# Layer 0 of a two-layer image kernel: VectorE's closing sum and statistics of each strip's second output half are moved one step later in its own instruction order

## What is computed

```python
def _L0_conv_ref(x, w_hidden, b_hidden, w_dw, b_dw, w_proj, b_proj, ln_w, ln_b):
    hidden = jnp.einsum('bchw,oc->bohw', x, w_hidden) + b_hidden[None, :, None, None]
    hidden = depthwise_3x3(hidden, w_dw) + b_dw[None, :, None, None]
    q, k, v = jnp.split(hidden, 3, axis=1)                  # 128 channels each
    q_fft = jnp.fft.rfft2(_to_patches(q))                   # patches of 8 by 8
    k_fft = jnp.fft.rfft2(_to_patches(k))
    out = _from_patches(jnp.fft.irfft2(q_fft * k_fft, s=(8, 8)))
    out = layernorm_over_channels(out) * ln_w + ln_b
    return jnp.einsum('bchw,oc->bohw', v * out, w_proj) + b_proj[None, :, None, None]

x = x + _L0_conv_ref(_gn(x), ...)      # _gn: group norm, 32 groups of 2 channels
x = x + _L1_conv_ref(_gn(x), ...)      # layer 1 needs the group statistics of layer 0's output
```

## Time and profile before

| what | before |
|---|---|
| median of 3 runs | 9162.08 us |
| the profiled execution's own time | 9166.47 us |
| its span | 9164.7 us |
| layer 0's loop (about 216 to 6476 us of the span) | 6260 us, 128 strips |
| TensorE busy, whole span | 8542.7 us (93%) |
| VectorE busy | 7484.3 us (82%) |
| ScalarE busy | 6350.6 us (69%) |
| GpSimd busy | 4819.6 us (53%) |
| mean granted TensorE clock | 0.985 of full speed |

### The profile page before, as it was taken

How to read it: one execution, slowest core, us unless ns; L and a number is a source line. 1 busy time by engine, 2 the same in 40 slices (tenths; PEclk the granted TensorE clock), 3 DMA queues, 4 the chain that set the end, 5 groups by cost and what they waited for, 6 DMA issues and landing times. The chain is left out here.

```text
span 9164.7 us, 170682 instructions
## 1 busy us (share of the span) xinstructions
PE 8542.7 (93%) x57838; PEld 4864.3 (53%) x57838; DVE 7484.3 (82%) x9864; ACT 6350.6 (69%) x8676; POOL 4819.6 (53%) x2752
## 2 busy tenths in 40 slices
PE   0999999999999999999999999999887999999999
PEld 0666666666666666666666666666432333333333
DVE  4788788788888878878887777778767999999999
ACT  0777777677777767777776777777406888888888
POOL 1444434344344344444443444434207999999999
PEclk9999999999999999999999999999998999999999
DMA  6122222222222222222212122122394555555555
GB/s 141 47 61 65 50 61 63 54 61 50 65 61 50 65 54 58 65 50 61 65 46 53 43 50 51 45 48 51 85 234 96 120 119 118 119 118 121 119 120 117
DMA packets 618296, 715.70 MB, mean 78 GB/s; under 512 B 44382, under 2 KB 577348, under 8 KB 594352
## 3 DMA queue, kind: packets, MB, share of 16 engines
q1 hardware_dynamic: 618160, 713.88, 33.4%
HBM read 549.03 MB, written 164.70 MB: 78 GB/s over the span
## 5 line engine op out<-in xcount | busy, mean ns | idle before, releaser
L633 PE MATMUL banks<-w_hi,hi_lo 128*128 128x256 f16 x18432 | 2407.1, 277 | 87.0 <-DVE hi_lo L935 87.0
L633 PEld LDWEIGHTS banks<-w_hi,hi_lo 128*128 128x128 f16 x18432 | 1760.3, 100 | 926.2 <-issue 523.7
L591 POOL TENSOR_TENSOR u_im<-q_im,k_swap 128x512 f32<-128x512 f32 x512 | 652.0, 1273 | 1834.4 <-ACT q_im L829 1747.5
L1442 POOL TENSOR_TENSOR part_sum<-part_sum,prod 128x1024 f32<-128x1024 f32 x660 | 1561.3, 2366 | 53.1
L967 DVE SCALAR_TENSOR_TENSOR v_s<-banks,tap_w,v_s 128x512 f32<-128x512 f32 x2048 | 1534.7, 749 | 54.6 <-ACT v_s L818 0.3
L1471 PE MATMUL banks<-z,conv_w 128*128 128x512 f32 x3128 | 1575.7, 619 | 0.0
L803 ACT ACTIVATE qk<-banks,inv_wscale 128x512 f32<-128x512 f32 x1024 | 706.4, 690 | 1221.2 <-PE banks L633 1215.7
L594 POOL TENSOR_TENSOR u<-u,u_im 128x512 f32<-128x512 f32 x512 | 726.4, 1419 | 1069.6 <-DVE u L944 1069.6
L633 PE MATMUL banks<-w_lo_pair,hi_pair 128*128 128x256 f16 x6144 | 1017.7, 275 | 0.0
L600 POOL TENSOR_TENSOR u<-u,u_mean 128x512 f32<-128x512 f32 x512 | 533.0, 1041 | 797.5 <-DVE u_mean L975 797.5
L944 DVE TENSOR_TENSOR u<-q_re,banks 128x512 f32<-128x512 f32 x512 | 349.6, 683 | 636.0 <-ACT q_re L831 635.7
(11 more groups left out here) (252 smaller groups left out, 15735.4 us busy)
## 6 DMA issues: line engine op xcount, KB each, us to landing
xr<-in_x_dram SPq DMA_DIRECT2D x258, 640.0 KB, 9.2
xb<-y_scratch SPq DMA_DIRECT2D x268, 320.0 KB, 4.7
xa<-y_scratch SPq DMA_DIRECT2D x268, 256.0 KB, 5.3
x_res<-in_x_dram SPq DMA_DIRECT2D x258, 256.0 KB, 4.0
out_dram<-res SPq DMA_DIRECT2D x258, 256.0 KB, 3.3
y_scratch<-ys SPq DMA_DIRECT2D x256, 256.0 KB, 3.9
yc<-y_scratch SPq DMA_DIRECT2D x256, 256.0 KB, 5.5
xs<-in_x_dram SPq DMA_DIRECT2D x92, 512.0 KB, 7.2
```

The lines of the kernel that those rows point to most:

```text
L591: nc.gpsimd.tensor_tensor(u_im[:], q_im[:], k_swap[:], ALU.mult).then_inc(u_made, 1)
L633: r = pe.matmul(out, px, w, start=n == 0, stop=n == 13)
L1442: nc.gpsimd.tensor_tensor(part_sum[:], prod[0][:] if n == 0 else part_sum[:], prod[n + 1][:], ALU.add)\
```

## The change

`finish` is cut in two behind L991. Its last two instructions, L994 and L996, with their waits and the signal `pair_ready`, become a function `output`. In step 0 of a strip (first half of the output) `output` is called right behind `finish`, as before. In step 2 (second half) it is no longer called there: it is called at the end of the next step, step 3, behind the last six `taps`. `high_stacks`, `both_stacks`, `product`, `times_v`, `taps` and `means` of step 3 now stand ahead of it. The end of the loop calls both halves in the order of before.

```diff
@@ -990,6 +990,13 @@
                     v.tensor_tensor(t_n[:], b_y[:], rs[:], ALU.mult)
                     v.scalar_tensor_tensor(out, b_var[:].rearrange("p (c r) -> p r c", r=R), b_proj[:, 0:1],
                                            x_res[sb_][:, :, GCOL * m:GCOL * m + GCOL], ALU.add, ALU.add).then_inc(fin_read, 1)
+
+                def output(i, k):
+
+                    m = ((k - 4) % 4) // 2
+                    sb_ = ((k - 4) // 4) % 2
+                    done = i * 4 + (k - 2) // 2
+                    out = ys[sb_][:, :, GCOL * m:GCOL * m + GCOL]
                     v.wait_ge(fin_read, done)
                     v.tensor_tensor(out, out, t_n[:].rearrange("p (c r) -> p r c", r=R), ALU.add).then_inc(fin_step, 1)
                     v.wait_ge(fin_step, done)
@@ -1067,8 +1074,12 @@
                             taps(i, k, 2, 8)
                         if stats and k == 4:
                             x_chunk(i)
+                        if k % 4 == 3 and not (first and k < 5):
+                            output(i, k - 1)
                         if k % 2 == 0 and not (first and k < 4):
                             finish(i, k)
+                        if k % 4 == 0 and not (first and k < 4):
+                            output(i, k)
                         if k % 4 == 2:
                             high_stacks(s, b)
                         if k % 4 == 0:
@@ -1079,8 +1090,10 @@
                     times_v(NB, 0, True)
                     means(NB, 0)
                     finish(NB, 0)
+                    output(NB, 0)
                     times_v(NB, 1, True)
                     finish(NB, 2)
+                    output(NB, 2)
```

## The result

The changed kernel takes 8866.99 us (median of 4 runs, 8863.69 to 8872.17) against 9162.82 us: ratio 0.9673, interval 0.9661 to 0.9684. That is 296 us less.

What follows compares the result with a forecast made beforehand. TensorE was taken to bound layer 0's loop. VectorE's chain shortens by 4.44 - 2.50 + 0.87 - 1.00 = 1.81 us; over 126 strips, less 2.7 us, that saves 225.4 us: 8937 us, range 8895 to 8988.

Steps and rivals of the forecast that it cites:

- What bounds layer 0: Layer 0's loop goes at TensorE's pace except for waits at inverse and the stacks, 2.08 us a strip.
- What is taken out, 4.44 us: VectorE, step 2: without L994 and L996 ahead of the stacks, L918 comes 4.44 us earlier.
- the hold handed to L918, 2.50: VectorE, step 2: GpSimd's L581 now holds L918 as it held L994, costing 2.50 us.
- L922 freed, 0.87: VectorE's L922 would be through before GpSimd's L591 and no longer held, giving back 0.87 us.
- the second hold on a copy, 1.00: GpSimd's L591 falls into L924 and the VectorE copy behind it waits, costing 1.00 us.
- What TensorE gets of it as wait: Step 3's chain moves with L944: TensorE's waits shrink by 1.81 us a strip, leaving 0.27 us at inverse.
- The new place, SyncE's queue: Output behind step 3's taps and pair_ready about 15.7 us later, delaying queued loads and store: cost 0 for both.
- Image boundaries: In 3 strips TensorE waits 5.6 us for VectorE's L1029; 0.9 us each off the gain, 2.7 us.
- TensorE gains 1.81 us per strip; the most it could is 2.08: TensorE in layer 0's loop: gain of 1.81 us a strip, capped by its waits of 2.08 us.
- Rival 1: The second hold does not happen, g is 2.81 us, both TensorE waits vanish: 8903 us; chance 0.2.
- Rival 2: Holds pile up: L918 3.37, copy 1.27 us, 9078 us; or L994 loses to L591, 9019 us; chance 0.11.
- Rivals 3 and 4: TensorE waits the same for ScalarE, 9162 us, chance 0.03; or late input load, 9477 us at 40 us landing, chance 0.03.

Runs made afterwards that it cites:

- e9: Changed kernel with the L918 pair (edge rows) taken out of step 2 and put at the end of step 1: 8833 us, ratio 0.9635.
- e11: e9 with the next image's variance computed in step 0 ahead of finish, output and masks, three times a run: 8817 us, ratio 0.9623.
- e12: Changed kernel with the late add (end of step 3) working on one of 64 columns, output not the reference's: 8860 us, ratio 0.9671.
- e6: Changed kernel with the first half's add and statistics moved too, to the end of step 1 behind its taps: 8863 us, ratio 0.9675.
- e2: Kernel before with only the statistics (L996) and their signal moved to the end of step 3, the add L994 left in step 2: 9030 us, ratio 0.9852.
- e5: Changed kernel with three useless GpSimd products of 1.04 us each ahead of step 3's less_mean: 9174 us, ratio 1.0007.
- e10: Kernel before, output untouched, with only the L918 pair moved to the end of step 1: 8939 us, ratio 0.9753.
- e1: Kernel before with the second half's output put behind high_stacks, still in step 2: 9131 us, ratio 0.9957.

## Why the prediction was wrong, point by point

*What bounds layer 0*: right. With the two waits gone, e9 and e11 leave TensorE nearly no wait in the loop.

*What is taken out, 4.44 us; the hold handed to L918, 2.50; L922 freed, 0.87; the second hold on a copy, 1.00*: right in kind and close in size. Measured are 2.42 (3.81 less 1.39), 0.87 and 0.98 (1.67 less 0.69). Sum 1.91 us against 1.81, and the chain in the timeline is 1.92 shorter. That L581 keeps its turn hung on a narrow margin, and here the forecast had luck: L581 starts 0.09 us ahead of L918, where it started 0.10 us ahead of L994. In nearly all strips it is 0.09 or 0.10 us.

*What TensorE gets of it as wait*: right. 228.5 us of idle time went in the loop (222 over the span), 225 were forecast. The 0.27 us left at `inverse` in each strip, 34 us in all, is 33.8 us. *The new place, SyncE's queue*: cost 0, right within 15 us, as e12, e6 and e2 show. *Image boundaries*: 0.9 us each was taken off, 1.5 is lost in wait.

*Where it failed*: the step "TensorE gains 1.81 us per strip; the most it could is 2.08". It takes TensorE's busy time as fixed, so that no more than its waits could be gained, and from that came both the forecast and the low end of 8895. But the wait of 1.8 us cost more than itself: in 42 of the strips TensorE's clock fell to half for some 3.4 us behind it, 1.65 to 1.8 us of lost time each, and with the wait these went too, all but one. e5 shows the link from one side (the wait alone brings them back), e10 from the other (another edit that shortens the wait drops them). That term is 72 us, put at nothing: 222 us of idle and 72 of busy time are the 294 us by which the profiled span is shorter. The idle part was forecast within 3 us.

The sign stood in the rows of before and was not read: the row of the loop's busy times gives a granted clock of 0.99, one hundredth of 6260 us, 63 us, or with the rounding anything from 31 to 94. In the kernel after the same figure is 1.00. The list of what would make the forecast wrong looked at waits alone.

Rival 1 (both waits vanish, 8903) and the others asked only how much wait goes. Rival 2's second form (L591 wins against the moved add) did not happen: the add arrives first. Its first form (both holds longer) did not happen either: they are 2.42 and 0.98. Rivals 3 and 4 did not come up: ScalarE still waits for TensorE, and L790 in the loop for no load.

## What to carry to other kernels

Where TensorE bounds a stage and has short regular waits, look for products of one shape that take longer behind some of the waits, and at the granted clock of the stage in hundredths: here a wait of 1.8 us cost another 1.7 us where the clock fell, about twice its length, and removing part of it (from 1.8 to 1.4 us here) can already bring the whole clock part back. When an instruction is held by another engine's (here L994 by GpSimd's L581), moving it can hand the hold to the next one in its order, as here to L918; count what leaves the chain and leave the hold in.

## What was not expected of the hardware

In these kernels the loss of clock rises steeply with the length of the wait: 1 to 3 of 128 strips at waits of 0.6 to 1.5 us, 28 to 57 at 1.8 to 1.9, 128 at 2.9 to 3.0. It isn't the length alone: before and e1 have the same waits at `inverse`, 1.76 to 1.84 us, and 43 and 28 strips, and e5 with 1.82 to 1.93 us has 57. The one strip in which the changed kernel still has a stretch, apart from the start, is the second: `inverse` waits 1.83 us there, at 271 us. Before, the stretches mostly come in every second strip, some 99 us apart and a few in a row, and then none for 200 to 390 us. Which of the strips are hit wasn't settled; no run varied the work around the wait at a fixed length.

When GpSimd and VectorE were in each other's way, the one that was waiting while the other ran got the next turn: L591, which came during L924, ran ahead of L925, which stood right behind L924 in VectorE's own order. The Trainium skill (page "SBUF — State Buffer", section on who interferes with whom) says that the order of issue decides who blocks. The trace agrees at both margins seen, 0.09 us in the changed kernel (L581 first) and 0.02 us in e9 (VectorE first).
